# Cross attention of a decoder layer: keys of two steps made in one 512-column product in every second step

## The chip, the cores and the metric

The kernel runs on one core of one Trainium2 chip. The metric is the device time of one execution in microseconds (us). The kernel before was timed in three runs; one more execution was recorded with the hardware profiler, and all times inside the program come from that one.

## What is computed

One decoder layer on 32 sequences of 64 tokens with 512 features (2048 tokens): a self attention against a cache, a cross attention against a context of the same shape, and a linear layer with a low-rank part, each with a residual and a layer norm. The change lies in the cross attention:

```python
def _L0_xattn_ref(query, kv, Wq, bq, Wkv, bkv, Wo, bo):
    NHEAD, NKV, HDIM = 32, 8, 128
    G = NHEAD // NKV
    q = (query @ Wq + bq).reshape(B, L, NKV, G, HDIM)
    k_, v_ = jnp.split(kv @ Wkv + bkv, 2, axis=-1)
    k = k_.reshape(B, Lk, NKV, HDIM)
    v = v_.reshape(B, Lk, NKV, HDIM)
    scores = jnp.einsum('blkgd,bmkd->bkglm', q, k) * scale
    attn = jax.nn.softmax(scores, axis=-1)
    o = jnp.einsum('bkglm,bmkd->blkgd', attn, v).reshape(B, L, NHEAD * HDIM)
    return o @ Wo + bo
```

## The kernel before

Every float32 operand of a matrix product is kept as two parts, a high one (`...h`) and a low one (`...l`), and each product is made of three matrix products (high by high, high by low, low by high; `split3`). After a product, ScalarE (ACT) reads PSUM and writes the high part, and then VectorE (DVE) reads the same PSUM bank and writes the low part.

The first stage (to about 1650 us) is the self attention, the second (to about 2760 us) the cross attention, the third the linear layer. The second stage is a loop of 64 steps, `n = 4 g + s`. The group `g` (0 to 15) stands for one of the 8 key/value heads in one half of the batch; `s` (0 to 3) for four of the 16 sequences of that half. The order of work is written out by hand, once for each engine. TensorE (PE) does in step n, in this order:

- `score2(n)`: 16 matrix products of 128 columns, queries against the keys `k2` (in the trace `big<-xk,xqh` and `big<-xk,xql`);
- `project2(n - 1, 0)`: the first half of the output projection of the step before, 12 products of 512 columns (`bank<-xwoh,xoh` and its two partners). It waits for `o_lo` of step n - 1, which is the low part of that step's attention output (`xol`), and for the four blocks of output weight, whose loads and splits are at s = 0;
- two `query2`: 24 products of 512 columns (`big<-yTh,wqTh` and partners);
- `turn2(n)`: four transposes of the normalised probabilities, which GpSimd (POOL) writes last (`P<-P,sm`);
- `project2(n - 1, 1)`: the other half of the projection;
- `values2(n)`: probabilities by values, 64 rows at a time (`big<-xph,xvh` and partners). ACT then writes `xoh` in two instructions and DVE `xol` in two, which is `o_lo` of step n;
- `key2(g + 1, s)`, for g up to 14: the keys of the next group for the same four sequences, 12 products of 256 columns (`big<-xTh,xwkh`, or `big<-xTh,wkvTh` where the key weight lies in the other buffer, and partners); ACT and DVE write them to `k2` (lines 1003 and 1441, `xk`);
- if g is odd, `value_rows2(g + 1, s)`: 24 products of 256 columns (`big<-xwvh,xTh` and partners). Step 0 makes value rows at this place too.

At s = 0 ACT and DVE also split the output weight (`xwoh`, `xwol`): two blocks ahead of `xoh` and `xol`, two behind the keys. Query, key and value products take turns in the two halves of one PSUM pair (`big0`); each waits until the product two places before it has been read.

```python
                values2(n)
                ...
                if g + 1 < GG:
                    key2(g + 1, s)
                    if g % 2 == 1:
                        value_rows2(g + 1, s)
```

Of the kernel before, what the change touches and what calls it, by code (L numbers as in the profile page):

```python
# [8 lines left out]
ALU = mybir.AluOpType  # L9
ACT = mybir.ActivationFunctionType  # L10
# [7 lines left out]
G = 8  # L18
# [11 lines left out]
HT = NT // 2  # L30
GG = 2 * G
# [225 lines left out]
Q_PLACE = query_places()  # L257


def pairs2(g, s):  # L260
    return [HT * (g // G) + 2 * s, HT * (g // G) + 2 * s + 1]

# [10 lines left out]
def f(ap):  # L273
    return ap.bitcast(F32)


def split3(ah, al, bh, bl):
    return [(ah, bh), (ah, bl), (al, bh)]


def decoder_kernel(nc, xt, x, ctxt, rope, wq_v, wk_v, wv_v, wo_v, k_cache, v_cache, block_idx,
                   wq2_v, bqk_in, wkv2_v, wo2_v, xbo, fw_v, fb, fa_v, fB, fp, out):
    with ExitStack() as top:
# [65 lines left out]
        bqk = sb("bqk", [128, 48])  # L349
# [105 lines left out]
        def wait_weight_free(gate, kind, n):  # L455

            if kind == "wq" and n >= 4:
                gate.wait_ge(q_done, (2 * ((n - 4) // 2) + 1, n % 2))
            elif kind == "xwq":
                gate.wait_ge(q_done, (2 * ((n + 60) // 2) + 1, n % 2))  # L460
            elif kind == "wo" and n >= 3:
                gate.wait_ge(wo_done, (2 * ((n - 3) // 2) + 1, 3))
            elif kind == "wk" and n >= 1:
                gate.wait_ge(tile_tr, ("vn", n - 1))
            elif kind == "wv":
                gate.wait_ge(tile_tr, ("kn", n))
            elif kind == "xwk":
                gate.wait_ge(tile_tr, ("vn", G - 1))
            elif kind == "x" and n >= HT:
                gate.wait_ge(q_done, (30 + (n - HT) // 4, 1))  # L470
            elif kind == "ctx" and n < HT:
                gate.wait_ge(q_done, (62 + n // 4, 1))
            elif kind == "ctx":
                gate.wait_ge(kv_done, ("v", G - 2, n % HT // 2))
                gate.wait_ge(kv_done, ("k", G - 1, n % HT // 2))
            elif kind == "fw":
                gate.wait_ge(kv_done, ("v", GG - 2, n // 2))
                gate.wait_ge(kv_done, ("k", GG - 1, n // 2))
            elif kind == "wq2" and n >= 4:
                gate.wait_ge(q_done, (2, 2 * (n // 4) - 1, n % 4))  # L480
            elif kind == "wo2" and n >= 4:
                gate.wait_ge(wo_done, (2, n - n % 4 - 1, 1))
            elif kind == "wk2" and n >= 2:
                gate.wait_ge(kv_done, ("k", n - 2, 3))
            elif kind == "wv2" and n >= 2:
                gate.wait_ge(kv_done, ("v", n - n % 2 - 2, 3))
            elif kind == "fa":
                gate.wait_ge(kv_done, ("v", GG - 2, 2))
                gate.wait_ge(kv_done, ("k", GG - 1, 2))
            elif kind == "fb":  # L490
                gate.wait_ge(kv_done, ("k", GG - 2, 3))

        def low_on_dve(kind, n):
            return (kind == "wo2" and n % 2 == 1) or (kind == "x" and (n < 6 or n >= HT and n % 2 == 0)) or (kind, n) in (("wq", 0), ("wq", 1), ("wk", 0), ("wv", 0))
# [64 lines left out]
        def sync_program(sp):  # L559
# [144 lines left out]
            sp.dma_start(xacc2[:, :, :], kept_x.rearrange("(t p) d -> p t d", p=128)).then_inc(in_x2("x"), 16)  # L704
            for i in range(6, len(TWO_LOADS)):
                load_two(i)
            gate.wait_ge(kv_done, ("k", GG - 1, 3))
            sp.dma_start(fbb[:, :], fb.rearrange("(a d) -> a d", a=1).to_broadcast([128, 512])).then_inc(
                in_fbb("fbb"), 16)
            for s in (in_bob, in_pcol, in_x2, *in_raw):  # L710
# [168 lines left out]
        def scalar_program(act):  # L879
# [119 lines left out]
            def key2_hi(g, s):  # L999
                gate.wait_ge(kv_done, ("k", g, s))  # L1000
                if g >= 1:
                    gate.wait_ge(s_done, (2, 4 * (g - 1) + s, 1))
                act.activation(k2[:, 4 * s:4 * s + 4, 0, :],
                               bank_at[("k", g, s)][:, 0:256].rearrange("p (b i) -> p b i", i=64), ACT.Identity,
                               bias=bqk[:, 32 + g % G:33 + g % G]).then_inc(kv_hi(("k", g, s)), 1)

            def value2_hi(g, s):
# [133 lines left out]
            for n in range(STEPS):  # L1141
                g, s = n // 4, n % 4
                work = blocks_at(g, s)
                last = n == STEPS - 1
                for bp in range(2):
                    gate.wait_ge(s_done, (2, n, bp))
                    if n >= 1:
                        gate.wait_ge(tile_tr, ("p2", n - 1))
                    act.activation(P2[:, bp].rearrange("p (x k) -> p x k", k=64),
                                   ps_sc[:, bp, :].rearrange("p (x a k) -> p x a k", a=2, k=64)[:, :, 1, :],  # L1150
                                   ACT.Copy).then_inc(sb_done((n, bp)), 1)
                for tt in early_x3(n):
                    tile_high("x3", tt)
                gate.wait_ge(max_done, (2, "sub", n))
                act.activation(flat(P2[:, :, :]), flat(P2[:, :, :]), ACT.Exp, scale=SCALE).then_inc(
                    exp_done((2, n)), 1)
                for tt in tiles_at(g, s):
                    weight2("ctx", tt)
                for m, j in units(n):
                    query2_hi(m, j)  # L1160
                for tt in tiles_at(g, s):
                    tile_high("x2", tt)
                gate.wait_ge(tile_tr, ("p2", n))
                if n >= 1:
                    gate.wait_ge(pv_done, ("v2", n - 1))
                act.activation(p2h[:, :], ps_tp, ACT.Copy).then_inc(tile_hi(("p2", n)), 1)
                if n == 0:
                    key2_hi(0, 3)
                if n == STEPS - 2:
                    low_rank_hi(0)  # L1170
                for a in work[:2]:
                    weight2(*a)
                gate.wait_ge(pv_done, ("v2", n))
                if n >= 1:
                    gate.wait_ge(wo_done, (2, n - 1, 1))
                for par in range(2):
                    act.activation(o2h[:, :, 64 * par:64 * par + 64],
                                   ps_ov[par].rearrange("p (x i) -> p x i", i=64), ACT.Identity,
                                   bias=bqk[:, 40 + g % G:41 + g % G]).then_inc(o_hi((2, n, par)), 1)
                if n == STEPS - 1:  # L1180
                    for i in range(3):
                        square_root(pairs2(g, i), 2)
                if n == 0:
                    value2_hi(0, 3)
                if g + 1 < GG:
                    key2_hi(g + 1, s)
                    if g % 2 == 1:
                        value2_hi(g + 1, s)
                for a in work[2:]:
                    weight2(*a)  # L1190
                if 4 <= n < 8:
                    square_root([HT + 2 * n - 8, HT + 2 * n - 7], 1)
                if g == G + 1:
                    square_root(pairs2(0, s), 2)
# [62 lines left out]
        def bank_order():  # L1257
# [6 lines left out]
            def put(key):  # L1264
                nonlocal turn
                at[key] = q_banks[turn % 2]
                turn += 1

            for n in range(STEPS):
# [13 lines left out]
                if n == 0:  # L1283
                    put(("v", 0, 3))
                if g + 1 < GG:
                    put(("k", g + 1, s))
                    if g % 2 == 1:
                        put(("v", g + 1, s))
            put(("w", STEPS - 1, 0))
# [7 lines left out]
        def vector_program(dve):  # L1297
# [140 lines left out]

            def key2_lo(g, s):
                gate.wait_ge(kv_hi, ("k", g, s))  # L1440
                dve.scalar_tensor_tensor(
                    k2[:, 4 * s:4 * s + 4, 1, :], bank_at[("k", g, s)][:, 0:256].rearrange("p (b i) -> p b i", i=64),
                    bqk[:, 32 + g % G:33 + g % G], f(k2[:, 4 * s:4 * s + 4, 0, :]), ALU.add, ALU.subtract).then_inc(
                        kv_lo(("k", g, s)), 1)

            def value2_lo(g, s):
# [154 lines left out]
            for n in range(STEPS):  # L1601
# [53 lines left out]
                if n == 0:  # L1655
                    value2_lo(0, 3)
                if g + 1 < GG:
                    key2_lo(g + 1, s)
                    if g % 2 == 1:
                        value2_lo(g + 1, s)  # L1660
                for a in work[2:]:
# [102 lines left out]
        def tensor_program(pe):  # L1764
# [245 lines left out]
                products(ps, terms, q_done, (2, m, j))  # L2010

            def key2(g, s):
                c0 = 256 * s
                wh, wl = wk_at(g)
                ps = q_bank(("k", g, s), (kv_lo, ("k", g, s)))
                wait_split(gate, "wk2" if g >= 1 else "xwk", g)
                for t in pairs2(g, s):
                    wait_split(gate, "ctx", t)
                terms = []
                for c in range(NC):  # L2020
                    w = slice(128 * c, 128 * c + 128)
                    terms += split3(wh[:, w], wl[:, w], xTh[:, c, c0:c0 + 256], xTl[:, c, c0:c0 + 256])
                products(ps[:, 0:256], terms, kv_done, ("k", g, s))

            def value_rows2(g, s):
                ps = q_bank(("v", g, s), (kv_lo, ("v", g, s)))
# [12 lines left out]
            def score2(n):  # L2039
                g, s = n // 4, n % 4  # L2040
                gate.wait_ge(q_lo, (2, n // 2, 3))
                gate.wait_ge(kv_lo, ("k", g, s))
                if n >= 1:
                    gate.wait_ge(sm_done, ("sum", n - 1, 1))
                else:
# [97 lines left out]
            for n in range(STEPS):  # L2143
# [23 lines left out]
                if n == STEPS - 1:  # L2167
                    linear(1)
                if g + 1 < GG:
                    key2(g + 1, s)  # L2170
                    if g % 2 == 1:
                        value_rows2(g + 1, s)
            project2(STEPS - 1, 0)
# [100 lines left out]
```

## Time and profile before

| | |
|---|---|
| median of three runs | 2852.09 us (2850.1 to 2853.28) |
| the profiled execution, its own time | 2844.57 us |
| its span, first to last instruction | 2842.5 us |
| TensorE busy | 2775.0 us (98%) |
| VectorE busy | 1810.1 us (64%) |
| ScalarE busy | 1512.3 us (53%) |
| GpSimd busy | 1515.6 us (53%) |
| mean granted TensorE clock | 0.997 of full speed |

The profile counts an engine as busy while an instruction of it runs. TensorE's instructions overlap, so what a product costs is read from the distance between the starts of instructions, not from their durations. `x24` in a row means so many instructions merged in it.

### The profile page before, as it was taken

The numbers are of one execution on the slowest core, as the hardware profiler recorded it, in microseconds if no ns is written. First come the engines' busy times: TensorE is split into PE (matmuls) and PEld (weight loads), VectorE is DVE, ScalarE is ACT, GpSimd is POOL, SyncE is SP. The second block draws the span as 40 slices with busy tenths as digits, with TensorE's granted clock in tenths as the row PEclk, the third lists the DMA queues.
The fourth block names the chain that finished last, engine by engine and source line by source line (L and its number), as shares of the span: only waits on it lengthen the run. The fifth ranks groups of instructions, "written<-read, shape, count | busy, mean of one in ns | idle before, by whom it ended". The sixth has DMA issues, their size and how long they took to land.

```text
span 2842.5 us, 64777 instructions
## 1 busy us (share of the span) xinstructions
PE 2775.0 (98%) x27264; PEld 2437.6 (86%) x27264; DVE 1810.1 (64%) x3253; ACT 1512.3 (53%) x3207; POOL 1515.6 (53%) x1299
## 2 busy tenths in 40 slices
PE   7999999999999999999999999999999999999997
PEld 6888888888888888888888888888888888888876
DVE  6666666666666666666666666655555566555577
ACT  6566665666565565555656544443434444343345
POOL 7788787788776666666666742122224222212125
PEclk9999999999999999999999999999999999999999
DMA  6323323323334231332222221111112111111111
GB/s 178 90 72 100 100 62 96 108 74 82 107 94 133 81 85 43 84 84 68 74 81 80 66 82 42 34 41 34 46 37 64 43 40 38 42 34 41 31 30 60
DMA packets 91482, 197.74 MB, mean 70 GB/s; under 512 B 20664, under 2 KB 21304, under 8 KB 89144
## 3 DMA queue, kind: packets, MB, share of 16 engines
q1 hardware_dynamic: 71480, 154.80, 19.2%
q10 hardware_dynamic: 17664, 34.61, 3.8%
q8 instruction: 215, 3.52, 0.5%
q0 software_dynamic: 2048, 4.20, 0.5%
q14 instruction: 75, 0.61, 0.1%
HBM read 176.78 MB, written 16.78 MB: 68 GB/s over the span
## 4 chain that ended last, share of the span: by engine, by line
PE 64%; DVE 23%; ACT 7%; issue 4%; ACTq 1%; DMA 1%; POOL 0%; SPq 0%; DVEq 0%
PE big L1776 28%; PE bank L1776 16%; PE bank L1868 12%; DVE nmx L1361 7%; DVE P L1367 5%; PE big L1848 3%; DVE xacc L1389 3%; PE big L1868 3%; DVE rall L1383 2%; DVE qTl L1356 2%; ACT qTh L891 2%; ACT P L936 1%; ACT pth L945 1%; ACT oTh L951 1%; PE bank L1769 1%
## 5 line engine op out<-in xcount | busy, mean ns | idle before, releaser
L775 POOL TENSOR_TENSOR ptl<-P,pth 128x576 fp32r<-128x576 f32 x512 | 726.0, 1436 | 160.8 <-ACT pth L945 159.8
L936 ACT ACTIVATE P<-big,nmx 128x576 f32<-128x576 f32 x512 | 379.3, 741 | 305.9 <-DVE nmx L1361 303.4
L1868 PE MATMUL bank<-pth,v 32*128 32x256 f32 x4608 | 425.2, 281 | 20.9 <-DVE xacc L1389 17.5
L1367 DVE STREAM_TRANSPOSE P<-P 128x576 f32<-128x576 f32 x512 | 386.7, 765 | 75.0 <-ACT P L936 74.8
L1868 PE MATMUL big<-pth,v 32*128 32x256 f32 x4608 | 426.5, 281 | 1.7 <-issue 1.6
L1868 PEld LDWEIGHTS bank<-pth,v 32*128 32x128 f32 x4608 | 387.2, 186 | 34.0 <-issue 33.8
L1361 DVE TENSOR_REDUCE nmx<-big 128x1 f32<-128x576 f32 x512 | 377.8, 748 | 5.3 <-PE big L1848 2.3
L945 ACT ACTIVATE pth<-P 128x576 fp32r<-128x576 f32 x512 | 347.6, 682 | 51.2 <-DVE P L1367 50.7
L1868 PEld LDWEIGHTS big<-pth,v 32*128 32x128 f32 x4608 | 361.0, 186 | 3.6 <-issue 3.5
L1868 PE MATMUL bank<-ptl,v 32*128 32x256 f32 x2304 | 355.1, 278 | 0.7 <-issue 0.7
L1868 PE MATMUL big<-ptl,v 32*128 32x256 f32 x2304 | 330.2, 278 | 0.0
L848 POOL TENSOR_TENSOR P<-P,sm 128x512 f32<-128x512 f32 x64 | 66.9, 1046 | 450.8 <-DVE sm L1623 450.8
L780 POOL TENSOR_TENSOR oTl<-rall,oTh 128x256 fp32r<-128x256 f32 x256 | 183.3, 738 | 163.4 <-ACT oTh L951 163.3
L510 POOL TENSOR_TENSOR wqTl<-raw,wqTh 128x512 fp32r<-128x512 f32 x126 | 162.1, 1297 | 185.3 <-ACT wqTh L505 184.3
L1868 PEld LDWEIGHTS bank<-ptl,v 32*128 32x128 f32 x2304 | 249.8, 186 | 1.0 <-issue 0.9
L1435 DVE SCALAR_TENSOR_TENSOR xql<-big,bqk,xqh 128x256 fp32r<-128x256 f32 x252 | 110.3, 479 | 209.9 <-ACT xqh L995 209.9
L951 ACT ACTIVATE oTh<-rall 128x256 fp32r<-128x256 f32 x256 | 93.5, 412 | 276.1 <-DVE rall L1383 276.1
L1848 PE MATMUL big<-kTh,qTh 128*128 128x288 f32 x1024 | 231.8, 308 | 7.7 <-ACT P L936 6.9
L1383 DVE TENSOR_TENSOR rall<-bank,rall 128x256 f32<-128x256 f32 x128 | 48.3, 420 | 289.5 <-PE big L1868 284.8
L995 ACT ACTIVATE xqh<-big,bqk 128x256 fp32r<-128x256 f32 x252 | 105.9, 471 | 233.4 <-PE big L1776 233.3
L1848 PEld LDWEIGHTS big<-kTh,qTh 128*128 128x128 f32 x1024 | 177.5, 189 | 58.0 <-issue 18.1
L1868 PEld LDWEIGHTS big<-ptl,v 32*128 32x128 f32 x2304 | 224.6, 186 | 0.3 <-issue 0.2
(270 smaller groups left out, 8174.1 us busy)
## 6 DMA issues: line engine op xcount, KB each, us to landing
rall<-kept_r ACTq DMA_DIRECT2D x64, 512.0 KB, 3.7
raw<-in_wo SPq DMA_DIRECT2D x64, 256.0 KB, 3.3
raw<-in_xWq SPq DMA_DIRECT2D x64, 256.0 KB, 2.7
raw<-in_xWo SPq DMA_DIRECT2D x64, 256.0 KB, 2.6
raw<-in_wq SPq DMA_DIRECT2D x62, 256.0 KB, 2.9
v<-kept_v SPq DMA_DIRECT2D x24, 448.0 KB
v<-kept_v SPq DMA_DIRECT2D x68, 128.0 KB, 3.1
raw<-in_xWkv SPq DMA_DIRECT2D x32, 256.0 KB, 2.7
```

Source lines behind the costliest of these rows:

```text
L510: engine.tensor_tensor(lo, split_source(kind, n), f(hi), ALU.subtract).then_inc(signal((kind, n)), 1)
L775: pool.tensor_tensor(third_columns(ptl, i), blocks_of(i), f(third_columns(pth, i)), ALU.subtract).then_inc(p_low(i), 1)
L780: pool.tensor_tensor(out_quarter(ol[:, :, :], a), rall_quarter(a), f(out_quarter(oh[:, :, :], a)), ALU.subtract).then_inc(o_low((k, a)), 1)
L936: act.activation(P[:, i % PSLOTS, :].rearrange("p (k n) -> p k n", k=2), ps_s[i % 2][:, :, 0:HALF], ACT.Exp, bias=nmx[:, i % 8:i % 8 + 1], ...
L945: act.activation(third_columns(pth, i), blocks_of(i), ACT.Copy).then_inc(p_hi(i), 1)
L951: act.activation(out_quarter(oh[:, :, :], a), rall_quarter(a), ACT.Copy).then_inc(o_hi((k, a)), 1)
L1361: dve.tensor_reduce(nmx[:, i % 8:i % 8 + 1], ps_s[i % 2][:, :, 0:HALF], AX.XY, ALU.max, negate=True).then_inc(max_done(i), 1)
L1367: dve.transpose(P[:, i % PSLOTS, :], P[:, i % PSLOTS, :]).then_inc(p_turned(i), 1)
L1435: dve.scalar_tensor_tensor(q2l[:, at[0], :, at[1]], ps[:, 256 * half:256 * half + 256].rearrange("p (b i) -> p b i", i=64), bqk[:, h:h + 1 ...
L1776: t = pe.matmul(dst, a, b, start=first and i == 0, stop=final and end)
L1848: m = pe.matmul(ps_s[i % 2][:, h, 0:HALF], l, r[:, HALF * h:HALF * h + HALF], start=j == 0, stop=j == 2)
L1868: m = pe.matmul(ps_o[a][:, 0:256], v[r, s, l, :], p[r, lo:hi + 1:hi - lo, block_of(b), :, :], start=first, stop=final)
```

## The change

The keys of a group's steps s and s + 1 (s even) are now made together. For all groups but the first, `key2` is only called in the steps with odd s, and there makes 512 columns: those of the step itself and of the one before it. The reads of PSUM by ACT and DVE follow: one of 512 columns in place of two of 256. The keys of group 0, made ahead of the loop, stay at 256 columns. Waits that named the keys of an even step now name those of the odd step behind it. The order in which products take turns in the two PSUM banks is counted again without the calls that are gone.

```diff
+def keys_of(g, s):
+
+    return "k", g, s if g == 0 else s | 1
+
+def key_columns(g):
+    return 256 if g == 0 else 512
+
+def first_block(g, s):
+
+    return 4 * s + 4 - key_columns(g) // 64
...
-                act.activation(k2[:, 4 * s:4 * s + 4, 0, :],
-                               bank_at[("k", g, s)][:, 0:256].rearrange("p (b i) -> p b i", i=64), ACT.Identity,
+                b0, n = first_block(g, s), key_columns(g)
+                act.activation(k2[:, b0:4 * s + 4, 0, :],
+                               bank_at[("k", g, s)][:, 0:n].rearrange("p (b i) -> p b i", i=64), ACT.Identity,
...
             def key2(g, s):
-                c0 = 256 * s
+                n = key_columns(g)
+                c0 = 256 * s + 256 - n
...
-                    terms += split3(wh[:, w], wl[:, w], xTh[:, c, c0:c0 + 256], xTl[:, c, c0:c0 + 256])
-                products(ps[:, 0:256], terms, kv_done, ("k", g, s))
+                    terms += split3(wh[:, w], wl[:, w], xTh[:, c, c0:c0 + n], xTl[:, c, c0:c0 + n])
+                products(ps[:, 0:n], terms, kv_done, ("k", g, s))
...
-                gate.wait_ge(kv_lo, ("k", g, s))
+                gate.wait_ge(kv_lo, keys_of(g, s))
...
                 if g + 1 < GG:
-                    key2(g + 1, s)
+                    if s % 2 == 1:
+                        key2(g + 1, s)
                     if g % 2 == 1:
                         value_rows2(g + 1, s)
```

TensorE, the end of step 10 (g = 2, s = 2) and the start of step 11, before; rows that repeat a pattern are left out:

```order
L1776 MATMUL big<-xph,xvl 128x256
L1776 MATMUL big<-xTh,xwkh 128x256 [waits q_lo]
L1776 MATMUL big<-xTl,xwkh 128x256
L1776 MATMUL big<-xTh,xwkl 128x256
...
L1776 MATMUL big<-xk,xqh 128x128 [waits sm_done]
L1776 MATMUL big<-xk,xql 128x128
...
L1776 MATMUL bank<-xwoh,xoh 128x512 [waits o_lo,acc_done]
```

The same place of TensorE in the changed kernel:

```order
L1795 MATMUL big<-xph,xvl 128x256
L1795 MATMUL big<-xk,xqh 128x128 [waits sm_done]
L1795 MATMUL big<-xk,xql 128x128
...
L1795 MATMUL bank<-xwoh,xoh 128x512 [waits o_lo,acc_done]
L1795 MATMUL bank<-xwol,xoh 128x512
```

The 12 key products are gone from between `values2` and `score2`; only the 16 score products are left ahead of the projection that waits for `o_lo`.

DVE, the end of step 8 (g = 2, s = 0) and the start of step 9, before:

```order
L510 TENSOR_TENSOR xwol<-raw,xwoh 128x512 [waits w_hi]
L1645 SCALAR_TENSOR_TENSOR xol<-big,bqk,xoh 128x8x64 [waits o_hi] x2
L1441 SCALAR_TENSOR_TENSOR xk<-big,bqk,xk 128x4x64 [waits kv_hi]
L510 TENSOR_TENSOR xwol<-raw,xwoh 128x512 [waits w_hi]
L1608 TENSOR_TENSOR P<-big,P 128x256 [waits sb_done] x2
```

And in the changed kernel:

```order
L524 TENSOR_TENSOR xwol<-raw,xwoh 128x512 [waits w_hi]
L1663 SCALAR_TENSOR_TENSOR xol<-big,bqk,xoh 128x8x64 [waits o_hi] x2
L524 TENSOR_TENSOR xwol<-raw,xwoh 128x512 [waits w_hi]
L1626 TENSOR_TENSOR P<-big,P 128x256 [waits sb_done] x2
L1630 TENSOR_REDUCE mx<-P 128x8 [waits sm_done]
```

What stood ahead of `xol` stands ahead of it still: a split of the output weight. The key instruction behind it is gone.

## Rows read from the trace of the kernel before

**Rows 1.** The page: busy time of each engine, share of the span.

```profile
PE 2775.0 (98%) x27264; PEld 2437.6 (86%) x27264; DVE 1810.1 (64%) x3253; ACT 1512.3 (53%) x3207; POOL 1515.6 (53%) x1299
```

**Rows 2.** Stages: us, PE, PEld, DVE, ACT, POOL busy (count), PEclk, DMA share, GB/s.

```profile
1650.00:2760.00 1110.00, 1104.95 (x6707) 948.78 (x6706) 645.94 (x1187) 475.38 (x951) 262.35 (x217) 1.00 0.14 43
1745.00:1765.00 20.00, 18.85 (x119) 16.14 (x117) 14.46 (x27) 10.82 (x20) 5.99 (x5) 1.00 0.17 54
```

**Rows 3.** Chain of waits, steps 33, 34 and 37: start us, us, what.

```profile
2251.55 4.28 PE big L1776 x40
2258.64 5.44 PE big L1776 x24
...
2318.72 7.16 PE big L1776 x64
```

**Rows 4.** Timeline of PE, step 34 to 35 (start us, us, instruction).

```profile
2267.90 0.28 PE L1776 MATMUL big<-xph,xvl 64*128 64x256 f32 x2
2268.11 0.39 PE L1776 MATMUL big<-xTh,xwkh 128*128 128x256 f32 x1
2268.34 0.28 PE L1776 MATMUL big<-xTl,xwkh 128*128 128x256 f32 x1
...
2269.66 0.22 PE L1776 MATMUL big<-xk,xqh 128*128 128x128 f32 x1
2269.72 0.28 PE L1776 MATMUL big<-xk,xql 128*128 128x128 f32 x1
...
2271.39 0.44 PE L1776 MATMUL bank<-xwoh,xoh 128*128 128x512 f32 x1
2271.68 0.40 PE L1776 MATMUL bank<-xwol,xoh 128*128 128x512 f32 x1
```

**Rows 5.** Timeline of PE: first and last of 24 query products, 512 columns.

```profile
2207.49 0.39 PE L1776 MATMUL big<-yTh,wqTh 128*128 128x512 f32 x1
...
2212.70 0.39 PE L1776 MATMUL big<-yTh,wqTl 128*128 128x512 f32 x1
```

**Rows 6.** Timeline of PE, step 60 to 61, where no keys are made.

```profile
2713.92 0.28 PE L1776 MATMUL big<-xph,xvl 64*128 64x256 f32 x2
...
2714.30 0.28 PE L1776 MATMUL big<-xk,xql 128*128 128x128 f32 x1
```

**Rows 7.** Timeline of ACT and DVE, step 34 (g = 8, s = 2).

```profile
2268.24 1.27 ACT L1177 ACTIVATE xoh<-big,bqk 128x512 fp32r<-128x512 f32 x2 [1.75 <-PE big L1776]
...
2268.96 1.41 DVE L1645 SCALAR_TENSOR_TENSOR xol<-big,bqk,xoh 128x512 fp32r<-128x512 f32 x2 [0.95 <-ACT xoh L1177]
...
2269.86 0.47 ACT L1003 ACTIVATE xk<-big,bqk 128x256 fp32r<-128x256 f32 x1 [0.35 <-PE big L1776]
...
2270.36 0.48 DVE L1441 SCALAR_TENSOR_TENSOR xk<-big,bqk,xk 128x256 fp32r<-128x256 f32 x1
```

**Rows 8.** Timeline of DVE and PE, step 32 (g = 8, s = 0).

```profile
2237.09 1.37 DVE L510 TENSOR_TENSOR xwol<-raw,xwoh 128x512 fp32r<-128x512 f32 x1 [0.55 <-ACT xwoh L505]
...
2238.38 1.40 DVE L1645 SCALAR_TENSOR_TENSOR xol<-big,bqk,xoh 128x512 fp32r<-128x512 f32 x2
...
2239.92 0.44 PE L1776 MATMUL bank<-xwoh,xoh 128*128 128x512 f32 x1
```

**Rows 9.** Timeline of DVE, PEld and PE: the projection of step 16 waits.

```profile
1962.85 0.69 DVE L510 TENSOR_TENSOR xwol<-raw,xwoh 128x512 fp32r<-128x512 f32 x1 [1.18 <-ACT xwoh L505]
...
1963.60 0.19 PEld L1776 LDWEIGHTS bank<-xwoh,xoh 128*128 128x128 f32 x1 [0.31 <-DVE xwol L510]
...
1963.94 0.39 PE L1776 MATMUL bank<-xwol,xoh 128*128 128x512 f32 x1
```

**Rows 10.** Timeline of DVE and PE, step 36 (g = 9, s = 0).

```profile
2301.31 1.40 DVE L1645 SCALAR_TENSOR_TENSOR xol<-big,bqk,xoh 128x512 fp32r<-128x512 f32 x2
...
2305.73 0.44 PE L1776 MATMUL bank<-xwoh,xoh 128*128 128x512 f32 x1
```

**Rows 11.** Timeline of POOL, step 34: the probabilities that the transposes wait for.

```profile
2260.28 1.05 POOL L848 TENSOR_TENSOR P<-P,sm 128x512 f32<-128x512 f32 x1 [7.41 <-DVE sm L1623]
```

More of the change, by code:

```diff
@@ L474, in wait_weight_free @@
                 gate.wait_ge(kv_done, ("v", G - 2, n % HT // 2))
-                gate.wait_ge(kv_done, ("k", G - 1, n % HT // 2))
+                gate.wait_ge(kv_done, keys_of(G - 1, n % HT // 2))
             elif kind == "fw":
                 gate.wait_ge(kv_done, ("v", GG - 2, n // 2))
-                gate.wait_ge(kv_done, ("k", GG - 1, n // 2))
+                gate.wait_ge(kv_done, keys_of(GG - 1, n // 2))
             elif kind == "wq2" and n >= 4:
@@ L483, in wait_weight_free @@
             elif kind == "wk2" and n >= 2:
-                gate.wait_ge(kv_done, ("k", n - 2, 3))
+                gate.wait_ge(kv_done, keys_of(n - 2, 3))
             elif kind == "wv2" and n >= 2:
@@ L488, in wait_weight_free @@
                 gate.wait_ge(kv_done, ("v", GG - 2, 2))
-                gate.wait_ge(kv_done, ("k", GG - 1, 2))
+                gate.wait_ge(kv_done, keys_of(GG - 1, 2))
             elif kind == "fb":
-                gate.wait_ge(kv_done, ("k", GG - 2, 3))
+                gate.wait_ge(kv_done, keys_of(GG - 2, 3))
         def low_on_dve(kind, n):
@@ L706, in sync_program @@
                 load_two(i)
-            gate.wait_ge(kv_done, ("k", GG - 1, 3))
+            gate.wait_ge(kv_done, keys_of(GG - 1, 3))
             sp.dma_start(fbb[:, :], fb.rearrange("(a d) -> a d", a=1).to_broadcast([128, 512])).then_inc(
@@ L1185, in scalar_program @@
                 if g + 1 < GG:
-                    key2_hi(g + 1, s)
+                    if s % 2 == 1:
+                        key2_hi(g + 1, s)
                     if g % 2 == 1:
@@ L1285, in bank_order @@
                 if g + 1 < GG:
-                    put(("k", g + 1, s))
+                    if s % 2 == 1:
+                        put(("k", g + 1, s))
                     if g % 2 == 1:
@@ L1440, in key2_lo @@
                 gate.wait_ge(kv_hi, ("k", g, s))
+                b0, n = first_block(g, s), key_columns(g)
                 dve.scalar_tensor_tensor(
-                    k2[:, 4 * s:4 * s + 4, 1, :], bank_at[("k", g, s)][:, 0:256].rearrange("p (b i) -> p b i", i=64),
-                    bqk[:, 32 + g % G:33 + g % G], f(k2[:, 4 * s:4 * s + 4, 0, :]), ALU.add, ALU.subtract).then_inc(
+                    k2[:, b0:4 * s + 4, 1, :], bank_at[("k", g, s)][:, 0:n].rearrange("p (b i) -> p b i", i=64),
+                    bqk[:, 32 + g % G:33 + g % G], f(k2[:, b0:4 * s + 4, 0, :]), ALU.add, ALU.subtract).then_inc(
                         kv_lo(("k", g, s)), 1)
@@ L1657, in vector_program @@
                 if g + 1 < GG:
-                    key2_lo(g + 1, s)
+                    if s % 2 == 1:
+                        key2_lo(g + 1, s)
                     if g % 2 == 1:
@@ L2016, in key2 @@
                 wait_split(gate, "wk2" if g >= 1 else "xwk", g)
-                for t in pairs2(g, s):
+                for t in range(HT * (g // G) + c0 // 128, HT * (g // G) + 2 * s + 2):
                     wait_split(gate, "ctx", t)
@@ L2169, in tensor_program @@
                 if g + 1 < GG:
-                    key2(g + 1, s)
+                    if s % 2 == 1:
+                        key2(g + 1, s)
                     if g % 2 == 1:
```

## The prediction

> **What bounds the kernel now.** I read the page first: TensorE is busy 98% of the span, no other engine over 64% [rows 1]. Then the stages: the cross attention is 1110 us, with 1104.95 us of TensorE, at the full clock (1.00, the 2.4 GHz level) [rows 2]. So a microsecond of TensorE's order here is a microsecond of the kernel, as long as nothing makes it wait. The chain of waits says the same: it runs through TensorE from product to product for whole steps [rows 3]. Last the timelines, for what each product costs between starts, and for how long before TensorE needs it each operand is ready.
>
> **What a key product costs.** 256 columns: the second key product of step 34 starts at 2268.34 and the first score product at 2269.66, 11 starts later: 0.120 us each. The piece of the chain behind `project2` has 64 products where there are value rows and 40 where not, 7.16 and 4.28 us [rows 3]: 2.88 us for 24, 0.120 again. 512 columns: the trace has no key product of that width; the nearest rows are the query products, also 128 by 128 weights with three parts in turn: 2207.49 to 2212.70 is 23 starts, 0.2265 us each [rows 5]. So 24 products of 256 cost 2.88 us and 12 of 512 cost 2.72 us: the wide form saves 0.16 us per pair of steps, no more. There are 30 pairs (15 groups, two each), 4.8 us in all.
>
> A rule weighs in here. The Trainium skill, page "TensorE: Matmul & The Clock Gate", section "Back-to-back issue gap", gives for products that each load their weights a sustained spacing of about 131 ns at 512 columns and 81 ns at 128. By that rule (an estimate) the wide key product would cost 12 x 0.131 = 1.6 us, hardly more than the narrow one now. The trace does not agree: its 512 columns take 0.2265 us [rows 5]. The sum goes by the row.
>
> **What the place costs.** The saving is not spread evenly. A step with even s loses its key product; one with odd s gets the wide one.
>
> *Odd steps, 30 of them:* 12 x (0.2265 - 0.120) = +1.28 us each. The first product behind `values2` has its extra 0.1 us either way (2268.11 to 2268.34 is 0.23 in place of 0.12 [rows 4]). Nothing is there to hide this behind: +38.4 us.
>
> *Even steps, 30 of them.* If nothing waits, 12 x 0.120 = -1.44 us. The bare passage is in the trace at step 60: from the last product of `values2` to the second score product 0.38 us without keys [rows 6], 1.82 us with them (2267.90 to 2269.72 [rows 4]); the difference is 1.44. But behind the 16 score products stands `project2(n, 0)`, which waits for `o_lo`: ACT reads the output of `values2`, DVE writes `xol`. Neither starts sooner by this change, since both start from `values2` and from what stood ahead of them before. The key product was what covered this latency.
>
> - Odd g, 14 steps, and step 0: `value_rows2` (2.88 us) is still there. At step 36 `xol` ends at 2302.71 and the projection starts at 2305.73 [rows 10]: 1.44 us sooner it still has 1.5 us to spare. Full saving: 15 x 1.44 = 21.6 us.
> - Even g, s = 2, 8 steps. At step 34 `xol` ends at 2268.96 + 1.41 = 2270.37 [rows 7]. Without the keys TensorE would reach the projection at 2271.39 - 1.44 = 2269.95 [rows 4], before it. How a wait on DVE ends is seen at step 16: `xwol` ends at 1963.54, the weight load behind it starts at 1963.60, the product after that at 1963.94 [rows 9]. So the first weight load would be at 2270.43 and the second product at 2270.77, where it was at 2271.68 [rows 4]: 0.91 us saved of 1.44. 8 x 0.91 = 7.3 us.
> - Even g, s = 0, the 7 steps with g = 2 to 14. Here DVE splits a block of the output weight before `xol`, 1.37 us. At step 32 `xol` ends at 2238.38 + 1.40 = 2239.78, and the projection started at 2239.92 [rows 8]: it was on the edge already. With the keys gone the load is at 2239.84 and the second product at 2240.18, before it was 0.29 behind 2239.92, at 2240.21. Saved: 0.02 to 0.03 us, 7 times, 0.2 us. Even without this wait the fourth block of output weight, which comes through a load and two splits, is no sooner: at step 16 it holds TensorE already [rows 9].
>
> *The other engines.* One read of 512 columns in place of two of 256 shortens their work, and they are not the bound. At the odd steps the key instructions get longer: from 0.47 and 0.48 us [rows 7] to about those of the other 512 columns, 1.27 and 1.41 us for two [rows 7], so some 0.2 us more on each. What would be late next is the softmax and the transposes. POOL ends the probabilities of step 34 at 2261.33 [rows 11]; TensorE asks for them behind the queries, at 2258.64 + 5.44 = 2264.08 [rows 3]. 2.7 us of cover, and 0.4 us is asked of it: nothing. If that cover were gone it would be 0.4 us at each of 30 steps, 12 us. The turns in the two banks give no wait: each product still has a whole other one, 1.4 us or more, between itself and the one whose read it needs.
>
> **The sum.** +38.4 - 21.6 - 7.3 - 0.2 = +9.3 us; with the roundings, +9.4. The profiled execution took 2844.57 us (span 2842.5): it would take 2854.0. The median of the three runs is 7.5 us higher, 2852.09; the difference is put on that: 2861.5 us, 0.33% slower.
>
> **The rivals.** About 0.2%, 5.7 us, is what a measurement of this kernel can tell from no change.
>
> 1. *No wait comes into being*, because ACT and DVE, with fewer instructions, or TensorE's run-ahead cover it. Then the sum is 38.4 - 30 x 1.44 = -4.8 us: 2847.3, within 0.2%. For it: TensorE has hardly waited at this place so far. Against: the ends of `xol` above do not depend on the keys. It decides if `xol` ended 0.5 us sooner at s = 2 and 1.4 us at s = 0. Chance 0.05. This is the case on the other side of my forecast.
> 2. *Only the steps with s = 2 escape*, where the margin is 0.5 us: 9.4 - 8 x 0.53 = +5.2 us, 2857.3. Chance 0.06, within 0.2%.
> 3. *The wide key product is cheap*, bounded by its weight loads and not its columns: no dearer than 12 x 0.120. Then the odd steps cost nothing, and the sum is 9.4 - 38.4 = -29 us: 2823. It speaks against it that the queries, with the same loads, do not do so [rows 5]. The cited page's spacing lies near this case. Chance 0.01. To it I add 0.01 for some gain that I don't see.
> 4. *Something else becomes late at the odd steps*, the transposes first: +12 us on top, 2873. The margin of 2.7 us speaks against it. Or the short waits lower the clock: the stretch with a 1.15 us wait of TensorE (18.85 us busy of 20) kept 1.00 [rows 2], and the new ones are of that size. Chance 0.04 for both.
>
> **How the numbers follow.** The forecast has 0.83: 2861.5 us. Its bounds: the s = 2 steps save between nothing and all (+7.3, -4.3 us), the 512-column product is within 0.03 us of the queries' (1 us), and medians of this kernel differ by 1 to 2 us. Range 2855 to 2868; it leaves out cases 1, 3 and 4 and is the likeliest case's own. Faster by over 0.2%: 0.02. Within 0.2%: cases 1 and 2 and a thin edge of the forecast, 0.13. Slower: 0.85.
>
> **What the profile of the changed kernel would show.** Key products of 512 columns 0.227 us apart. In the steps of even g, TensorE idle ahead of `bank<-xwoh,xoh`, released by DVE `xol`: 7 times about 1.3 us (s = 0) and 8 times 0.3 to 0.5 us (s = 2), some 12 us together, where there was none. Pieces of the chain through `xoh` and `xol` there. Even steps of odd g 1.44 us shorter, the two steps where TensorE already waits for POOL, 5 and 37, with the same wait. Odd steps 1.28 us longer. Clock unchanged. I am wrong if the wait for `xol` is absent, if the wide products are not 0.227 us apart, or if TensorE waits at the transposes.

## The result, and the profile after

| | before | changed |
|---|---|---|
| median, six runs each | 2852.69 us | 2872.43 us |
| lowest to highest | 2850.1 to 2857.84 | 2868.57 to 2875.62 |
| profiled execution, span | 2842.5 us | 2873.5 us |
| second stage in it, first score product of step 0 to that of step 63 | 1075.87 us | 1092.65 us |

The ratio is 1.0064 (95% interval 1.0052 to 1.0076): slower by 0.64%, some 18 us, where the forecast was 0.33% and 9.4 us. The direction held; the time lies outside the range. On a second chip the same kernel gave 1.0042 (1.0028 to 1.0056), and on a third one execution of each took 2872.35 and 2849.62 us.

The page of the changed kernel: TensorE has 12.6 us more busy time with 360 products fewer [rows 1], and no other engine has more work.

```profile
span 2873.5 us, 63984 instructions
PE 2787.6 (97%) x26904; PEld 2430.4 (85%) x26904; DVE 1803.6 (63%) x3223; ACT 1502.3 (52%) x3177; POOL 1513.7 (53%) x1299
```

The two spans differ by 31.0 us, but only 16.8 of them lie in the stage that was changed. Step 0 began at 1682.85 us, before at 1668.42; the first stage has the same instructions. In the other profiles of this study it began between 1666.2 and 1669.4 us on one chip and between 1675.5 and 1680.6 on two others. On one of these two the kernel before, with only a query product moved, began it at 1678.0. So 14 us of the 31 are taken for spread of the first stage (the chips of the first two profiles are not on record). The second stage took 1075.87 and 1075.45 us in two profiles of before, and is what the experiments are read by.

The waits of TensorE in the second stage, changed kernel (us in total, times, longest). Before there was none of the second line and one of 0.3 us of the first; the third is as before. A wait "at s = 0" or "at s = 2" is named by the step whose output is waited for; it stands in the step behind, ahead of the projection.

```profile
PE bank L1795 <- issue: 8.9, 8, 1.2
PE bank L1795 <- DVE xol L1663: 3.2, 8, 0.4
PE bank L1788 <- POOL P L862: 2.3, 2, 1.1
```

The second line is the forecast wait at s = 2, eight times 0.4 us. The first holds the seven at s = 0, 1.2 us each, and the short one of before; there the profile names no releaser, but the timeline of step 32 and 33 shows DVE's `xol` ending at 2261.37 and the projection behind it, as in [rows 8]:

```profile
2259.97 1.40 DVE L1663 SCALAR_TENSOR_TENSOR xol<-big,bqk,xoh 128x512 fp32r<-128x512 f32 x2
2261.47 0.76 PE L1795 MATMUL bank<-xwoh,xoh 128*128 128x512 f32 x1 [1.22 <-issue]
2262.03 0.63 PE L1795 MATMUL bank<-xwol,xoh 128*128 128x512 f32 x1
```

The last two rows are the surprise. These products take 0.63 us and stand 0.43 us apart (the next starts at 2262.46), not 0.40 and 0.23. The windows give the reason (us, PE, PEld, DVE, ACT, POOL busy, granted clock, DMA share, GB/s): first the end of step 16 and the wait, then the 3.4 us behind it, then on; and the same stretch behind step 32.

```profile
1974.00:1978.00 4.00, 2.78 (x28) 2.53 (x26) 3.08 (x4) 2.60 (x5) 2.55 (x2) 1.00 0.31 79
1978.00:1981.40 3.40, 3.40 (x10) 2.58 (x10) 2.21 (x5) 1.17 (x3) 0.00 (x0) 0.52 0.65 169
1981.40:1985.00 3.60, 3.60 (x17) 2.97 (x16) 2.01 (x4) 0.63 (x1) 1.04 (x1) 0.98 0.13 51
...
2261.40:2264.80 3.40, 3.33 (x8) 2.68 (x9) 1.87 (x4) 1.17 (x3) 0.27 (x1) 0.50 0.53 175
```

Behind three of the seven waits at s = 0 the granted clock fell to 0.50, the 1.2 GHz level, for some 3.4 us. In all 13 such cases of this study the fall came between 0.3 us before the projection started again and 0.4 us after. The chain shows what one costs: in step 33 the projection behind the wait took 4.56 us, in step 35, behind the shorter wait, 3.00 with its restart.

```profile
2257.41 2.84 PE big L1795 x28
2260.25 1.22 issue
2261.47 4.56 PE bank L1795 x12
...
2291.77 0.94 PE big L1795 x12
2292.71 0.03 issue
2292.73 0.70 ACT xoh L1192
2293.43 0.03 issue
2293.45 1.42 DVE xol L1663 x2
2294.88 0.14 issue
2295.01 3.00 PE bank L1795 x12
```

At the shorter wait the chain leaves TensorE for `xoh` and `xol`; before, it stayed on TensorE there [rows 3].

Step lengths (from one step's first score product to the next, from the timeline of TensorE), steps 8 to 15:

| g, s | 2, 0 | 2, 1 | 2, 2 | 2, 3 | 3, 0 | 3, 1 | 3, 2 | 3, 3 |
|---|---|---|---|---|---|---|---|---|
| before | 15.73 | 15.73 | 15.72 | 15.73 | 18.61 | 18.60 | 18.61 | 18.61 |
| changed | 14.18 | 18.65 | 14.20 | 17.77 | 17.18 | 19.95 | 17.17 | 19.95 |

The even group loses 1.9 us in four steps, without half clock; the odd group gains 0.2.

### The profile page after: what moved, and what is told of

It reads as the page before. It is cut to its first block, busy times and chain, and to the rows that moved or that the text cites. A ratio compares the mean times of both kernels' runs of the same rounds, so it can differ in the third digit from the quotient of the medians.

```text
span 2873.5 us, 63984 instructions
## 1 busy us (share of the span) xinstructions
PE 2787.6 (97%) x26904; PEld 2430.4 (85%) x26904; DVE 1803.6 (63%) x3223; ACT 1502.3 (52%) x3177; POOL 1513.7 (53%) x1299
## 4 chain that ended last, share of the span: by engine, by line
PE 68%; DVE 20%; ACT 6%; issue 4%; ACTq 1%; DMA 1%; POOL 0%
PE big L1795 28%; PE bank L1795 18%; PE bank L1887 11%; DVE nmx L1378 6%; PE big L1867 5%; DVE P L1384 4%; PE big L1887 4%; DVE xacc L1406 3%; DVE rall L1400 2%; DVE qTl L1373 2%; ACT qTh L905 2%; ACT P L950 1%; ACT pth L959 1%; ACT oTh L965 1%; PE bank L1788 1%
## 5 line engine op out<-in xcount | busy, mean ns | idle before, releaser
L1887 PE MATMUL bank<-pth,v 32*128 32x256 f32 x4608 | 431.0, 282 | 23.1 <-DVE xacc L1406 15.5
L524 POOL TENSOR_TENSOR wqTl<-raw,wqTh 128x512 fp32r<-128x512 f32 x126 | 162.0, 1296 | 187.9 <-ACT wqTh L519 186.0
L1867 PEld LDWEIGHTS big<-kTh,qTh 128*128 128x128 f32 x1024 | 178.2, 189 | 57.6 <-issue 17.8
```

The source lines that it names most:

```text
L524: engine.tensor_tensor(lo, split_source(kind, n), f(hi), ALU.subtract).then_inc(signal((kind, n)), 1)
L1867: m = pe.matmul(ps_s[i % 2][:, h, 0:HALF], l, r[:, HALF * h:HALF * h + HALF], start=j == 0, stop=j == 2)
L1887: m = pe.matmul(ps_o[a][:, 0:256], v[r, s, l, :], p[r, lo:hi + 1:hi - lo, block_of(b), :, :], start=first, stop=final)
```

## The experiments

**The two halves of the change.** Wide keys only where value rows follow, and only where they do not:

```diff
+def wide(g):
+    return g > 0 and g % 2 == 0      # the other kernel: g % 2 == 1
 def key_columns(g):
-    return 256 if g == 0 else 512
+    return 512 if wide(g) else 256
...
-                    if s % 2 == 1:
+                    if s % 2 == 1 or not wide(g + 1):
```

> Wide keys only where value rows are made at the same place too (steps of odd groups, keys of even groups); elsewhere two products of 256 columns as before. Theory A: no wait for the output's low part, 14 pairs that save 1.44 and cost 1.35 us, second stage -1.3 us against before (1074.6), ratio 0.999 to 1.001. Rival B (the wide product itself, or its longer reads, costs what was lost, wherever it stands): 14 of 30 pairs lose half of the 17 us, second stage about +8 us, ratio 1.003. Rival C: ratio as for the full change, 1.006.

> The other half alone: wide keys only in the steps of even groups, where no value rows follow. Theory A: 16 wide products at +1.35, step 0 at -1.44, eight s = 2 steps at -0.87, seven s = 0 steps at about 0 and some half-clock stretches at 1.5 us each: second stage +13 to +20 us, nearly all of the loss of the full change, ratio 1.005 to 1.007. Rival B: about half of the loss, +9 us, ratio 1.003.

Measured: under the value rows 0.9999 (0.999 to 1.0008), second stage 1075.02 us, 0.85 below before; uncovered 1.005 (1.0036 to 1.0064), second stage 1093.94 us, 18.1 above before. Of this, 1.7 us are a half-clock stretch in step 61, at a wait that the kernel before has too; two stretches followed s = 0 waits. All of the loss is in the uncovered half. The wide product costs the same in both (2.89 us), so rival B falls.

**The changed kernel again, twice.**

> The changed kernel once more, for a second profile and a comparison on this chip. In its first profile the second stage (first score product of step 0 to first of step 63) took 1092.65 us against 1075.87, and in three of the seven s = 0 steps of even groups the wait for the output's low part was followed by some 3.4 us of projection at half clock, about 1.5 us lost each. Theory A (the key products had covered the latency of the output's low part; the waits, and the clock after them, are the loss): again ratio 1.005 to 1.008, the waits of 0.5 us (s = 2) and 1.4 us (s = 0) at the same 15 places to 0.05 us, but the half-clock stretches at other steps and in another number, and the second stage at 1088 to 1098 us accordingly. Rival C (the loss is largely in the first stage, whose start was 14 us later in the first profile though the change touches nothing there): the first stage stands again 10 us or more above the 1668 us of before.

> The changed kernel's third profile, for the count of half-clock stretches. Two profiles had three each behind the seven waits of s = 0 (1.2 us idle), none behind the eight waits of s = 2 (0.3 us idle), none behind the 1.15 us waits of steps 5 and 37 at the transposes. Theory A: one to five of seven again, none at the other two kinds of wait, second stage 1088.2 us plus 1.45 us for each. Rival (the stretches were chance of those runs, or any wait can start one): none at s = 0, or some at the other waits.

Measured: 1.0042 (1.0028 to 1.0056), second stage 1092.51 us, three half-clock stretches behind s = 0 waits (steps 8, 24, 56); then 1093.71 us, again three there (8, 24, 48) and one in step 61. The waits stood at the same 15 places. In step 61 TensorE waits 1.75 us for `yTl`, in the kernel before too. There, in the third profile, are the last product ahead of the wait, the first one behind it, and the window behind:

```profile
2746.36 0.40 PE L1795 MATMUL bank<-xwoh,xol 128*128 128x512 f32 x1
2748.52 0.50 PE L1795 MATMUL big<-yTh,wqTh 128*128 128x512 f32 x1 [1.76 <-DVE yTl L1319]
2749.10:2752.50 3.40, 3.40 (x10) 2.64 (x8) 1.50 (x4) 0.00 (x0) 1.04 (x1) 0.50 0.00 0
```

**The wait covered.** TensorE's order alone:

```diff
-                project2(n - 1, 0)
-                for m, j in units(n):
+                ahead = g % 2 == 0 and s % 2 == 1
+                if ahead:
+                    query2(*units(n)[0])
+                project2(n - 1, 0)
+                for m, j in units(n)[ahead:]:
                     query2(m, j)
```

> The full change, with one of the two query products of the odd steps of even groups put ahead of the first half of the projection (TensorE's order alone): 2.7 us of other work between the scores and the wait for the output's low part. Theory A: the 15 waits and the half-clock stretches go, 30 pairs save 1.44 and cost 1.35 us, and the odd waits of before for the fourth block of output weight (0.5 us in all) go too: second stage 1072 to 1075 us, 18 to 20 us under the full change, ratio to before 0.998 to 1.000. If the later projection makes the softmax late instead (DVE adds it between the maximum and the sum), TensorE waits at the transposes, with a margin of about 1 us by the profile of before. Rival B: the loss stays, ratio 1.006.

Measured: 1.0001 (0.9992 to 1.001), second stage 1077.56 us: 15.1 us of 16.8 are back, with the same 30 wide products. No half-clock stretch. It did not reach 1075: each of these 16 steps now has a new wait of 0.2 us at the transposes, and step 21 one of 0.8 us for a block of output weight (`PE bank L1795 <- DVE xwol L524: 0.8, 1, 0.8`). The timeline of DVE, GpSimd and TensorE in step 11 of this kernel shows it:

```profile
1867.19 0.69 DVE L1479 TENSOR_TENSOR xacc<-bank,xacc 128x512 f32<-128x512 f32 x1 [3.13 <-PE bank L1795]
1867.80 0.68 DVE L1639 TENSOR_REDUCE sm<-P 128x8 f32<-128x512 f32 x1
1868.51 0.20 DVE L1641 RECIPROCAL sm<-sm 128x8 f32<-128x8 f32 x1
...
1868.79 1.04 POOL L862 TENSOR_TENSOR P<-P,sm 128x512 f32<-128x512 f32 x1 [5.87 <-DVE sm L1641]
...
1869.89 0.33 PE L1788 MATMUL bank<-ident,P 128*128 128x128 f32 x1
```

DVE's order puts the sum of the projection in the middle of the softmax. DVE idles 3.13 us for it, GpSimd ends at 1869.83, and the transposes start 0.06 later.

**And the sum moved.** The same kernel, DVE adding the projection behind the row sums in these steps:

```diff
-                if n < STEPS - 4:
+                later = n >= STEPS - 4 or g % 2 == 0 and s % 2 == 1
+                if not later:
                     add_out2(n - 1, 0)
...
-                if n >= STEPS - 4:
+                if later:
                     add_out2(n - 1, 0)
```

> The full change with one query product ahead of the projection, and now DVE also adds the projection behind the row sums of the softmax instead of ahead of them. In the run with the query product alone the transposes of those steps came 0.2 us late: DVE idled 3.1 us in the middle of the softmax for the later projection, and GpSimd's last step ended 0.06 us before the transposes. Theory A: that wait goes, the second stage falls by a further 3 to 4 us to 1073 to 1075 us, under before by 1 to 3 us; ratio 0.998 to 1.000. Rival: something else than the softmax sets those transposes, then it stays at 1077.6 us.

Measured: 0.9994 (0.9985 to 1.0003), second stage 1073.67 us: 2.2 us below before and 3.9 below the last one. Of the 3.9, the eight steps with s = 3 give 1.9 (17.15 us each, before 17.39) and the eight with s = 1 only 0.5, since waits of up to 0.4 us at the transposes are left there; 1.0 is the wait of step 21, which did not come this time. It is the best version found, about what the products alone are worth (30 x 0.09 = 2.7 us); the interval includes no change. Moving the sum in the kernel before, with the query ahead, was not tried.

**Control: the query ahead in the kernel before.**

> The kernel before with the same query product ahead of the projection in the odd steps of even groups, as a control for the run that did so in the changed kernel. Theory A: there is no wait for the output's low part to cover here, so nothing is gained, and the transposes of those steps come late as in that run: second stage 1075.9 - 0.5 (waits for the fourth block of output weight) + 1 to 4 = 1076 to 1079 us. Rival (the query product ahead is a gain of its own, and that run's 15 us came from it and not from the covered waits): the second stage falls under 1070.

Measured (one execution, 2859.44 us, where before took 2849.62): second stage 1081.34 us, 5.5 above before, beyond what I expected: the odd steps of even groups, 16 of them, are 15.95 to 15.97 us where they were 15.73 to 15.94 (+3.1 together), and a half-clock stretch made step 61 2.1 us longer. The query ahead is a cost by itself. What it gave in the changed kernel came from the waits it covered.

**The split behind the low part.** In the even groups at s = 0, DVE writes `xol` first:

```diff
-                for a in work[:2]:
-                    weight2(*a)
+                xol_first = g % 2 == 0 and s == 0
+                if not xol_first:
+                    for a in work[:2]:
+                        weight2(*a)
...
+                if xol_first:
+                    for a in work[:2]:
+                        weight2(*a)
```

> The full change, but at s = 0 of the even groups DVE writes the output's low part before it splits the second block of output weight (before: behind it). That split took 1.35 us with GpSimd busy beside it, and stood ahead of the low part. Theory A (the s = 0 waits are long because of this split): the low part ends 0.8 us sooner and the projection starts so much sooner at the seven steps, the wait shrinks from 1.4 to some 0.5 us, but part comes back as a wait for the second or the fourth block of output weight inside the projection; 0.3 to 0.8 us gained per step, 2 to 5 us in all, and with shorter waits fewer half-clock stretches (up to 4.5 us more): ratio to before 1.001 to 1.004. Rival: the fourth block holds the projection's end anyway, so the total per step is unchanged and only the half-clock stretches, if they need one long wait, go: 1.002 to 1.004; if they do not need it, 1.005.

Measured: 1.0051 (1.0037 to 1.0064), second stage 1089.92 us. The waits of the steps from 1690 to 2720 us:

```profile
PE bank L1800 <- DVE xwol L524: 4.1, 7, 0.6
PE bank L1800 <- issue: 3.7, 7, 0.5
PE bank L1800 <- DVE xol L1665: 3.2, 8, 0.4
```

Scores and projection together took 2.53 + 3.69 = 6.22 us, where the full change without half clock has 3.22 + 2.85 to 3.04: the wait ahead of the projection shrank by 0.7 us and a wait for a weight block came up inside it. So the rival's mechanism is right here: the blocks of output weight hold the end of the projection. One half-clock stretch was left, of seven chances. The ratio is above both ranges that went with fewer stretches (to 1.004): the full change without any is 12.5 us, 1.0044, by the table below, so these ranges were set too low.

**The wide product in the even steps.**

```diff
+def made_at(g, s):
+    return [(g, 3)] if s == 0 and g >= 1 else [(g + 1, 1)] if s == 2 and g + 1 < GG else []
...
-                if g + 1 < GG:
-                    if s % 2 == 1:
-                        key2(g + 1, s)
+                for gk, sk in made_at(g, s):
+                    key2(gk, sk)
+                if g + 1 < GG:
                     if g % 2 == 1:
                         value_rows2(g + 1, s)
```

> The same wide key products, but made in the even steps: keys of the next group's steps 0 and 1 at s = 2, keys of this group's steps 2 and 3 at s = 0 (s = 0 is where the long wait was). The odd steps lose theirs. Theory A: in even groups the odd steps save 0.87 us each (16 steps) behind a wait of 0.5 us, no wait of 1.4 us and no half-clock stretch, the even steps cost 1.35; odd groups as in the full change; one wide product moves to group 15. Second stage +4 to +8 us against before, 9 to 12 us under the full change, ratio 1.001 to 1.003. Rival B (the wide product itself is the cost): as the full change, 1.005 to 1.006.

Measured: 1.0007 (0.9998 to 1.0016), second stage 1079.48 us, 3.6 above before. The outputs of the odd steps of even groups are waited for as those of s = 2 were in the changed kernel, 0.4 us each, 15 times of 16, with no long wait among them (`PE bank L1799 <- DVE xol L1667: 6.0, 15, 0.4`), and no half-clock stretch was seen. It is less than the 4 us at the lower end, since the product that moved to step 60 also covers part of a wait that step 61 has in every other kernel (15.85 us, not 17.8; the wait is 0.55 us and not 1.75). The place of the product is worth 13 us, of which some 4 are half clock and 1.2 are this wait.

**Wide keys behind the value rows.** In the odd steps of odd groups `value_rows2` first, then `key2`, on all three engines.

> The full change, but in the odd steps of odd groups the wide key product stands behind the value rows instead of ahead of them. In every profile so far the 12 wide products behind the probabilities' product took 2.89 us, 0.34 to the second and 0.232 between the rest, where the prediction had 2.82 and 0.2265. During them ScalarE and then VectorE read the output from PSUM. Theory 1 (the spacing is stretched by what stands just ahead and beside: the 64-row products and the output's reads): behind the value rows the 12 take 2.72 to 2.79 us. Theory 2 (the spacing belongs to the product's own operands): 2.84 us or more. The other odd steps, of even groups, stay at 2.89.

Measured (one execution, 2872.85 us): 2.75 us for the twelve, 2.89 in the other odd steps. First and last of one such product, and then one of the full change:

```profile
1816.03 0.40 PE L1801 MATMUL big<-xTh,wkvTh 128*128 128x512 f32 x1
1816.27 0.40 PE L1801 MATMUL big<-xTl,wkvTh 128*128 128x512 f32 x1
...
1818.55 0.39 PE L1801 MATMUL big<-xTh,wkvTl 128*128 128x512 f32 x1
```

```profile
1991.82 0.50 PE L1795 MATMUL big<-xTh,xwkh 128*128 128x512 f32 x1
1992.16 0.40 PE L1795 MATMUL big<-xTl,xwkh 128*128 128x512 f32 x1
...
1994.48 0.39 PE L1795 MATMUL big<-xTh,xwkl 128*128 128x512 f32 x1
```

Behind the value rows the spacing from the second to the last is 2.28 / 10 = 0.228 us, close to the queries' 0.2265 [rows 5]. Behind the 64-row products it is 2.32 / 10 = 0.232, with 0.34 to the second. The product's own operands are not the cause: `wkvTh` and `xwkh` both have 0.232 behind the 64-row products. But little is gained by moving it: the value rows, now first, take 2.98 us in place of 2.87, so these steps are only 0.04 us shorter (19.91 and 19.95 us). The 0.1 us behind the 64-row products goes to whoever stands there. Whether the 64-row products ahead or the reads by ScalarE and VectorE beside cause it was not separated.

**A before once more,** for the first stage.

> The kernel before, profiled a second time, to see how much of the 14 us by which the first stage of the changed kernel was later is spread of the first stage itself. Theory A: the first score product of step 0, at 1668.4 in the first profile of before and at 1675 to 1683 in the five profiles since, stands between 1668 and 1683 here too; the second stage is again 1075.9 us to 1 us, with no half-clock stretch behind a wait in it except by chance. Rival C (the first stage is slower in the changed kernels for a cause of its own, such as where the instructions lie): the first stage is again at 1668 to 1670.

Measured (one execution, 2841.81 us): step 0 at 1666.16 us, second stage 1075.45 us, no half-clock stretch. 1666.16 lies below both ranges, nearer to rival C's; but on the same chip three changed kernels began step 0 at 1667.8 to 1669.4 us, and on the third chip the kernel before with the query ahead began it at 1678.0, between changed kernels at 1678.6 and 1680.4. Most of the difference goes with the chip; a share of 2 us or so that goes with the kernel isn't excluded.

## Why the prediction was half right

The second stage, term by term (us; measured from the first profile pair):

| term | predicted | measured |
|---|---|---|
| 30 wide products in place of narrow ones | +38.4 (1.28 each) | +40.5 (2.89 - 1.54 = 1.35 each) |
| 15 even steps with cover | -21.6 | -21.6 |
| 8 steps, s = 2 | -7.3 (0.91 each) | -6.8 (0.85) |
| 7 steps, s = 0, without the clock | -0.2 | 0.0 |
| half clock behind three of these | 0 | +4.3 (1.4, 1.5, 1.4) |
| a wait for the fourth weight block, step 21 | 0 | +0.4 |
| sum | +9.3 | +16.8 (stages: +16.8) |

- *The cost of the forms* held: the spacing of the queries carried over to within 2.5%. Mis-sized was the term of the wide product, by 0.07 us thirty times, because it took the spacing of a product that stands elsewhere. That is 2.1 us. By the prediction's own sign (0.227 us apart) this reading failed, though by little.
- *The cover* held: the key product had hidden ACT's and DVE's work on the output, and the waits are where and as long as forecast. Shown by the halves, by the query put ahead, and by the even-step kernel.
- *The clock* is the step that failed. The prediction put it at nothing in the sum, and as the second half of rival 4 at a part of 0.04. It said "the stretch with a 1.15 us wait of TensorE (18.85 us busy of 20) kept 1.00, and the new ones are of that size". Of that size they are, but the inference from one kind of wait to another did not hold. Over all profiles, 13 of 35 waits at s = 0 (five profiles; 1.22 us, one 1.50) were followed by half clock, none of 26 at the transposes of steps 5 and 37 (1.15 us), none of 63 of 0.4 us. One of the seven steps with the waits of 0.5 and 0.6 us in `xol_first` was followed by it, and in 4 of 12 profiles step 61's wait of 1.6 to 1.8 us. At s = 0 it is 1.4 to 1.5 us each, 4 us a run. With it the second stage alone gives 2852.1 + 16.8 = 2868.9 us, just outside the range; without it 12.5 us and 2864.6, inside.
- *The softmax cover* of rival 4 was there: the transposes came later in no step of the changed kernel than they had before. It was used up only when the projection was moved by a query product.
- The rest, between 16.8 us in the second stage and the 19.7 us between the medians, is within the spread of the first stage. The two ratios of the changed kernel (18 and 12 us) lie on both sides of 16.8; the interval of the second, 8 to 16 us, ends just below it, and no kernel of before was profiled on that chip.

Rivals 1 to 3 did not come about; of rival 4 the transposes did not, the clock did. Why the stretches follow some s = 0 waits and not others stays open. The DMA traffic beside them is not it: behind the wait of step 8, with the clock at 1.00, it was as high as behind the one of step 32, and behind the one of step 61, with 0.50, there was none. The window behind step 8:

```profile
1838.60:1842.00 3.40, 3.31 (x14) 2.66 (x15) 1.97 (x4) 1.18 (x3) 0.29 (x1) 1.00 0.63 187
```

## What to carry to other kernels

When two narrow products become one wide one, the saving is what leaving out one narrow product gives, less what the wide one takes beyond the other, here 1.44 - 1.35 = 0.09 us a pair. What the narrow product covered by standing where it stood was worth 0.6 us at s = 2 and 1.4 us at s = 0, before the clock. Before removing work from a full engine, find the next instruction on it that waits for another engine, and subtract. And don't read the clock's reaction to a wait from one or two other waits of about the same length: here 1.15 us never lowered it and 1.22 us did in 13 cases of 35. Which property of a wait or of the work around it decides was not shown.

## What the runs showed of the hardware that I had not expected

- A wait of 1.2 us in a stream at full clock was followed by 3.4 us at a granted clock of 0.50 in 13 of 35 cases. Ahead of it the engine had 12 products on 64 rows and 16 of 128 columns, 0.11 us apart. The waits at the transposes, 1.15 us idle, stand behind 24 products of 512 columns at full rate, and none of 26 was followed by it. Work of that kind ahead is no safeguard, though: the wait of step 61 (1.6 to 1.8 us) stands behind 12 products of 512 columns, 0.23 us apart, and was followed by 0.50 in 4 of 12 profiles.
- The same 512-column products were 0.228 us apart in one place and 0.232 in another; in both places the first product behind the 64-row products had an extra 0.1 us.
- The first stage, with the same instructions in all kernels, ended (by the start of step 0) at 1666.2 to 1669.4 us on one chip and 1675.5 to 1680.6 on two others (1682.9 in the profile whose chip is not on record); the second stage of the changed kernel differed by less than 1.3 over three profiles.
